# The 64-by-64 products of a linear attention unit in one stretch, the value projection behind them

## The reference

```python
qkv = jax.nn.silu(hidden_states @ qkv_w.T)
# per head, over blocks of tokens, with a state of 64 x 64:
aw = jnp.einsum('bhid,bhjd->bhij', qi, ki) * dd          # scores, decayed
intra = jnp.einsum('bhij,bhjd->bhid', aw, vi)            # within the block
inter = jnp.einsum('bhid,bhde->bhie', qi * qd_, state)   # carried by the state
new_state = state * bd_ + jnp.einsum('bhsd,bhse->bhde', ki * kd_, vi)
# over all heads:
attn = _rmsnorm(attn, norm_w)
gate = jax.nn.sigmoid(hidden_states @ gate_w.T)
return gate * attn @ out_w.T
```

## Time and profile before

| | us |
|---|---|
| median of 3 runs | 1164.99 |
| lowest, highest | 1161.36, 1165.12 |
| the profiled execution | 1165.4 |
| its span | 1162.7 |
| TensorE busy (matmuls) | 1106.1, 95% of the span |
| TensorE weight loads | 856.7, 74% |
| VectorE, ScalarE, GpSimd | 610.4, 618.9, 479.2 |

### The profile page before, as it was taken

How to read it: one execution, slowest core, us unless ns; L and a number is a source line. 1 busy time by engine, 2 the same in 40 slices (tenths; PEclk the granted TensorE clock), 3 DMA queues, 4 the chain that set the end, 5 groups by cost and what they waited for, 6 DMA issues and landing times. The chain is left out here.

```text
span 1162.7 us, 33305 instructions
## 1 busy us (share of the span) xinstructions
PE 1106.1 (95%) x14272; PEld 856.7 (74%) x14272; DVE 610.4 (52%) x1361; ACT 618.9 (53%) x1166; POOL 479.2 (41%) x513
## 2 busy tenths in 40 slices
PE   5999999999999999999999899897899999998898
PEld 4888888888888888888888688785344444435787
DVE  6143434243434454545445735799777777742643
ACT  3543434343435454545455676443567667675663
POOL 1354454453544554645544448401122222221246
PEclk9999999999999999999999999999999999998999
DMA  3100101001001001011022200184022232000001
GB/s 127 54 3 3 54 3 47 10 2 48 16 2 61 16 29 68 30 63 35 16 88 88 83 1 1 42 222 132 2 57 56 56 56 57 2 2 1 1 19 55
DMA packets 15951, 49.58 MB, mean 43 GB/s; under 512 B 2433, under 2 KB 7105, under 8 KB 13121
## 3 DMA queue, kind: packets, MB, share of 16 engines
q1 hardware_dynamic: 15808, 47.50, 14.3%
HBM read 36.54 MB, written 10.75 MB: 41 GB/s over the span
## 5 line engine op out<-in xcount | busy, mean ns | idle before, releaser
L1668 DVE TENSOR_REDUCE aa_mx<-aa_S 128x1 f32<-128x640 f32 (+1 forms) x192 | 177.0, 954 | 46.8 <-PE aa_S L1463 43.8
L1599 ACT ACTIVATE aa_PT<-aa_ST 128x512 f32<-128x512 f32 (+1 forms) x304 | 158.8, 579 | 73.0 <-PE aa_ST L1489 70.1
L500 DVE SCALAR_TENSOR_TENSOR la_y<-la_g,la_O 128x512 f32<-128x512 f32 x64 | 41.1, 683 | 224.2 <-PE la_O L678 224.2
L590 PE MATMUL la_R<-a_hTh,WF 128*128 128x512 f32 x384 | 130.9, 406 | 4.3 <-DVE a_hTl L147 4.3
L1395 POOL TENSOR_SCALAR_AFFINE_SELECT aa_PT<-aa_PT 128x256 f32<-128x256 f32 (+1 forms) x112 | 48.6, 440 | 181.0 <-ACT aa_PT L1599 180.7
L298 POOL TENSOR_TENSOR la_yl<-la_y,la_yh 128x512 fp32r<-128x512 f32 x62 | 79.3, 1302 | 92.1 <-ACT la_yh L376 92.1
L285 POOL TENSOR_TENSOR la_qd<-q,la_C 128x512 f32<-128x512 f32 x64 | 81.0, 1285 | 80.9 <-PE la_O L678 80.6
L507 DVE TENSOR_TENSOR X<-la_R,X 128x512 f32<-128x512 f32 x64 | 44.2, 691 | 121.8 <-PE la_R L590 121.7
L1460 PE MATMUL aa_S<-aa_stacks 96*128 96x512 bf16 (+3 forms) x384 | 98.4, 331 | 8.2 <-DVE aa_mx L1668 7.4
L1489 PE MATMUL aa_ST<-aa_stacks 99*128 99x512 bf16 (+3 forms) x384 | 99.4, 328 | 3.7 <-ACT aa_PT L1599 1.6
L341 ACT ACTIVATE la_v<-la_R 128x512 f32<-128x512 f32 x64 | 38.2, 598 | 114.4 <-PE la_R L590 114.4
(11 more groups left out here) (224 smaller groups left out, 2790.4 us busy)
## 6 DMA issues: line engine op xcount, KB each, us to landing
la_Wraw<-w_quads_dram SPq DMA_DIRECT2D x7, 1280.0 KB, 6.1
aa_stacks<-k_parts SPq DMA_DIRECT2D x16, 256.0 KB, 6.8
q_parts<-aa_QP SPq DMA_DIRECT2D x4, 768.0 KB, 4.1
aa_stacks<-q_parts SPq DMA_DIRECT2D x8, 384.0 KB, 4.7
k_parts<-aa_KP SPq DMA_DIRECT2D x4, 768.0 KB, 3.5
qw_w<-w_ffn_dram SPq DMA_DIRECT2D x12, 192.0 KB, 2.5
q_ffn<-qw_w SPq DMA_DIRECT2D x12, 192.0 KB, 1.9
X<-hidden_dram SPq DMA_DIRECT2D x4, 512.0 KB, 7.4
```

Of the source, the lines that this page charges most:

```text
L590: m = pe.matmul(out, a, b, start=n == 0, stop=n == len(pairs) - 1)
L1599: act.activation(PT[:, (NM2 * g + b) % NPT, h:h + nh, 0:w], ST[at % NB][:, 0:nh * w].rearrange("p (h q) -> p h q", h=nh), ACT.Exp, scale=S ...
L1668: dve.reduce_max(out, src, AXX).then_inc(s1_free, 1)
```

## The change

TensorE: `state_sums` and `scores` pair 1 move ahead of v's projection and ahead of the second `within`, which itself moves ahead of v. The wait that v's halves had is now one wait on `n0` before `scores` pair 1. In the last turn's units 6 and 7 the blocks without v move in the same way. ScalarE: the eviction of v's second half moves behind the two copies yh. No instruction of any engine is added or dropped, apart from waits.

```diff
@@ act, unit(i, j, last) @@
                 if has(last, j, 2):
-                    for n in range(2):
-                        evict(*step(i, j + 2), "v", n, n0 + n)
-                    n0 = n0 + 2
+                    evict(*step(i, j + 2), "v", 0, n0)
                 for pr in range(2):
                     act.wait_ge(y_ok, 16 * i + 2 * j + pr + 1)
                     act.activation(zh[:, pr, :], y[:, pr, :], ACT.Copy).then_inc(yh_ok, 1)
+                if has(last, j, 2):
+                    evict(*step(i, j + 2), "v", 1, n0 + 1)
+                    n0 = n0 + 2
@@ pe, unit(i, j, last) @@
                     scores((j + 2) % 8, (0,))
+                if has(last, j, 1):
+                    pe.wait_ge(kd_ok, 32 * i + 4 * j + 8)
+                    state_sums((j + 1) % 8)
+                if has(last, j, 2):
+                    pe.wait_ge(silu_ok, n0)
+                    scores((j + 2) % 8, (1,))
+                pe.wait_ge(half_ok, 8 * i + j + 1)
+                within(j, False).then_inc(o_ok, 1)
                 if has(last, j, 2):
                     for n in range(2):
-                        pe.wait_ge(silu_ok, n0 + n - 1)
                         project(*step(i, j + 2), "v", n)
                     n0 = n0 + 2
-                pe.wait_ge(half_ok, 8 * i + j + 1)
-                within(j, False).then_inc(o_ok, 1)
                 if last and j == 7:
                     outputs(i, 6, last, evicted(i, 6, last) + 2)
...
-                if has(last, j, 1):
-                    pe.wait_ge(kd_ok, 32 * i + 4 * j + 8)
-                    state_sums((j + 1) % 8)
-                if has(last, j, 2):
-                    scores((j + 2) % 8, (1,))
```

## The result

The changed kernel takes 1188.7 us (median of 4 runs, 1186.3 to 1191.1), the kernel before in the same measurement 1164.0 (1161.4 to 1165.1). The ratio is 1.0212, with a 95% interval of 1.0187 to 1.0237: 2.1% slower. The profiled execution, the fastest of the four, took 1186.3 us with a span of 1184.4, where the kernel before had 1162.7.

What follows compares the result with a forecast made beforehand. The prediction took TensorE's own instruction stream to bound the kernel. It summed 1165.4 - 10.8 (tile size) + 1 (ScalarE) + 0.6 (tail) + 29.7 (blocks) - 0.4 (profiled run to median) = 1185.5, say 1186 us; range 1163 to 1202.

Steps and rivals of the forecast that it cites:

- Changes of tile size, 0.36 us a unit: TensorE leaving v and entering g: two changes of tile size go, 10.8 us less over 30 units.
- ScalarE, +1 us: v's second eviction, now behind yh, slightly delays g's second half: 0 to 3 us over 30 units, 1 taken.
- The tail, +0.6: Unit 30, projecting no v: state_sums before the second within delays the last unit's products, 0.6 us more, bounds 0 and 0.93.
- Blocks, +29.7: Long small-product stretch: TensorE waits for its next 256-instruction block in 27 of 30 units, 1.15 us each; bounds 14 and 47.
- Rival 1: TensorE's instruction supply is deep enough, the two old gaps are accidents; only tile-size changes count: 1155.8 us, faster; 15%.
- Rival 2: Instruction blocks stall TensorE about a third as much, 0.35 us a unit: 1166 us, no change; 6%.
- rival 3: ScalarE becomes the bound: v's second eviction 0.3 us later, g's second half waits: 1164 us without the blocks; 2%.
- rival 4: TensorE's clock granted half for one period per unit, 51 us more: 1207 us; 2%.

Runs made afterwards that it cites:

- Run 1: Changed kernel with only TensorE's new order; ScalarE as before, both v evictions ahead of the yh copies: 1194.1 us, ratio 1.026.
- Experiments 4: Changed kernel plus 128 semaphore increments nobody waits for on TensorE's queue before the first unit, shifting all block edges by half a block: 1191.5 us, ratio 1.0238.
- 6: Changed kernel plus 84 or 67 semaphore increments per unit among wide products, 58 before the first unit; edges at 148, 404, 660: 1207.9 us, ratio 1.0371.
- 8: Changed kernel plus semaphore increments, at most 1.5 behind a matmul of g and k; edges at 32, 288, 544: 1172.0 us, ratio 1.0067.
- Experiment 7: Kernel before the change plus 84 or 67 semaphore increments per unit among wide products, as a control for their cost: 1196.6 us, ratio 1.0269.
- 10: New order in units with j mod 4 of 1 or 2, the order before in the others, plus 335 semaphore increments in all: 1170.7 us, ratio 1.007.
- run 5: Changed kernel plus 84 or 67 semaphore increments per unit among wide products, 174 before the first unit; edges at 32, 288, 544: 1178.0 us, ratio 1.0112.

## Why the prediction was right

Forecast 1186, measured 1188.7 (2.1% slower, where 1.8% was said).

- **Changes of tile size, 0.36 us a unit.** Holds. Units without a gap last 18.82 to 18.92 us, 0.35 to 0.48 less than before. For all 29: 30.4 us of gaps (the 30.2 and 0.2 in unit 11) less 0.3 for the old gap in unit 25, less the 19.9 by which they grew, is 10.2, 0.35 a unit. The rule of the Trainium skill on changes of mode ("TensorEngine Tiling (Array Packing)", Key Properties) had the direction right; what one costs the trace had to say.
- **ScalarE, +1 us.** v's second eviction ends at 80.18, and g's second half starts at about 80.66 (79.26 + 6 x 0.233); no wait on it is to be seen. yh's two took 1.14 us and not 1.23, and each starts 0.1 before the one ahead of it ends, which I had counted end to end. So 0, within the bounds. Run 1 shows what the step would have been without the edit: 4.6 us. I had looked only for the bank of g's second half; k's wait for g's first eviction was the nearer one.
- **The tail, +0.6.** Unit 30 is 0.63 us longer.
- **Blocks, +29.7.** 27 units x 1.15 were forecast, 25 with a mean of 1.25 were found: 31.2 against 31.0. The count was a bit high, since the stretch's first 300 positions are safe, not 285. The size was low, since the block comes 2.2 to 2.8 us after its packet starts and not always 2.25. (The 1.05 us at 536.5 were counted from the start of the unit; from the first start in the block ahead it is 0.7 there, as in most of the gaps.) That the two errors cancel to 0.2 us is luck; the mechanism is not. By Experiments 4, 6 and 8 the gaps follow the edges, with work and order unchanged, and by Experiment 7 the start of the packet decides where the position leaves it open.
- **What the sum lacks.** 2.1 us behind unit 31, where nothing was changed; the spread between runs of the same kernel is of that size. The medians differ by 24.7 us and the two profiled spans by 21.7, since the profiled execution was the fastest of its four; the other 3 us are in no trace.
- **Rival 1** needed an edge inside the stretch to cost under 0.36 us. It costs 0.7 to 1.7. The Trainium skill's sentence that crossing a 16 KiB block is mostly hidden ("Runtime: NRT & Kernel Launch", Instruction fetch mechanics) describes the wide products here, at 60 ns an instruction and more, and not the small ones, at 7.3. Its ground, that the sequencer issues more slowly than the memory fills, is what fails: 256 small ones last 1.9 us, and from the first start of a block until its successor is usable it took 2.9 to 3.7 us in the gaps. **Rival 2** (a third as much) fell with that, **rival 3** needed ScalarE to be late, **rival 4** a clock below 1.00, and the earlier trace rows and its counterpart after both show 1.00.

## What to carry to other kernels

Count a stretch of very short TensorE instructions in instructions, not in microseconds: in units 0 to 28 an edge up to 299 instructions into the long stretch cost nothing or up to 0.7 us, and from 300 on each edge of a 256-instruction block inside the stretch cost some 1.2 us, over three times what leaving out a pair of changes of tile size gives back. How much is safe depends on what runs ahead of the stretch: behind v's 3 us alone, an edge 235 to 241 instructions into it cost 0.5 to 1.1 us in the even units of run 7, and nothing in the odd ones. A few wide matmuls between two stretches of small ones are not only work, they are the time in which the next block arrives. Two gaps without a releaser, a whole number of blocks apart, in an otherwise full engine tell of this before a change makes it the rule; and a test that shifts all instructions by half a block moves such gaps and leaves the work alone.

## What the runs showed that I had not expected

- A semaphore increment on TensorE's queue is not free: 1.5 behind a matmul of 0.23 us hide, two cost 0.3 to 0.4 us over the 24 matmuls of g and k (run 5; 0.5 to 0.7 in run 7), and one behind each of the 24 matmuls of the out projection costs 0.6 to 0.9 us in even units and 0.1 to 0.3 in odd ones (run 8), where 20 behind the 24 cost 0.1 or nothing (run 5). What makes these differences was not tested.
- The kernel before is nearer the limit than it looks: its second stretch of 256 has positions at which an edge costs 0.5 to 1.1 us (run 7).
- In unit 29 packets start later than in the others: 0.9 to 2.2 us are lost at edges that cost the other units 0 to 0.7 (runs 5, 8 and 10). From the packet's start to TensorE's going on it is 2.3 to 2.7 us there as well. Why they start late is open.
